# A vision-transformer tokenizer on one Trainium2 core: the unit's steps in another order on TensorE, VectorE, GpSimd and SyncE

## The chip, the cores and the metric

The kernel runs on one NeuronCore of one Trainium2 chip. The metric is the device time of one execution in microseconds (us), lower is better. Engines are named PE (TensorE), DVE (VectorE), ACT (ScalarE), POOL (GpSimd) and SP (SyncE, which issues the DMAs). Each engine runs its own instructions in program order, and they wait for each other through semaphores that only count upwards.

## The reference

The program is a tokenizer for 64 images of 64 channels and 64 by 64 pixels, then a linear oscillator scan over 256 tokens per image, a GELU/SiLU mixing, a mixture of experts, and two layer norms. The change touches only the tokenizer, which is this:

```python
x = features.reshape(b, c, h, s, w, s)                # s = 4: patches of 16 pixels
reduce_feats = x.mean((3, 5)).reshape(b, c, hw).transpose(0, 2, 1)
unf = x.transpose(0, 1, 2, 4, 3, 5).reshape(b, c, hw, n).transpose(0, 2, 3, 1)
q = _ln(reduce_feats, ln_q_w, ln_q_b) @ Wq.T
kv = _ln(unf, ln_kv_w, ln_kv_b) @ Wkv.T
attn = jax.nn.softmax(jnp.einsum('bhpd,bhpnd->bhpn', q * scale, k), axis=-1)
aggre = jnp.einsum('bhpn,bhpnd->bhpd', attn, v)
aggre = aggre.transpose(0, 2, 1, 3).reshape(b, hw, c)
return reduce_feats + aggre @ proj_w.T + proj_b
```

Each patch's mean is the query, its 16 pixels are keys and values, and the result is projected and added to the mean.

## The kernel before, in words

The tokenizer takes 32 units (`UNITS`) of two images each, one image in partitions 0 to 63, the other in 64 to 127. A unit's pixels (2 MB) lie in one of four slots (`NF`) of `arena`, seen as `x[:, m, b, c]`: two halves b of four chunks c of 512 columns. Step n works on four units at once: it makes keys and scores of unit n+1, values of unit n, the projection of unit n-1, and means, squares and query of unit n+2. The order is written out by hand for each engine.

PE, step n (L1020 ff.), in program order: `keys(n+1, c)` for c = 0 to 3 (four matmuls each, into slot c % 2 of a ring of two PSUM buffers), `project(n-1, part)` for part = 0, 1, 2 (16 matmuls each, reading `prodv` of unit n-1), `scores(n+1)`, `values(n, k)` for k = 0 to 3 (same ring, slot k % 2), and for unit n+2 `pixel_squares`, `query` and `pixel_means`. Below, K0 to K3, P0 to P2, S, V0 to V3, SQ, Q and MS stand for these groups. Their waits:

- K2 and K3 wait until DVE has taken K0 and K1 from the ring (`keys_times_q`); S waits for all four key products.
- V0 waits for the third key product of unit n+1 (ring slot 0 was K2's), V1 for the fourth; V2 and V3 wait for the value products of V0 and V1 (`values_weighted`).
- P0 waits for all four value products of unit n-1; P2 waits for `pixels_added`, POOL's four additions of unit n-1.
- Q waits for `tokens_ready` of unit n-1, since both lie in the PSUM tile `qp`.

DVE, step n (L1475 ff.): four `key_products(n+1, c)` (KP0 to KP3), `tokens(n-1)`, `score_scale(n+1)`, `score_max(n+1)`, `value_products(n, 0)` and 1 (VP0, VP1), `score_sum(n+1)`, `query_var(n+2)`, `score_inverse(n+1)`, VP2, `query_scaled(n+2)`, VP3, `pixel_var(n+2)`. `prodv`, the result of the value products, has one buffer: VP0 of unit n may overwrite it only once P2 of unit n-1 has read it. That is one line of `value_products`:

```python
                if k == 0:
                    dve.wait_ge(projected_mm, u)
```

`projected_mm` counts the P2 groups that are done, so with u = n this is P2 of unit n-1. `tokens(n-1)` waits for the same count.

POOL, step n (L605 ff.): `patch_sums_first(n+2)` (waits for the pixels of that unit), `add_pixels(n-1, 2)` and `(n-1, 3)`, three smaller sums, `shift_scores(n+1)` (waits for `score_max`), `add_pixels(n, 0)`, `weigh_scores(n+1)` (waits for ACT's exponential), `add_pixels(n, 1)`, `norm_scores(n+1)`. `add_pixels(u, k)` needs VPk of unit u.

SP, step n: eight DMAs of 256 KB that spread the weights of unit n+1 over the partitions (`spread_weights`, from `wgt` to `wbc`, after `norm_scores`), then two DMAs of 1 MB that load unit n+4, which wait for V3 of unit n. ACT's order is not touched: for a unit it has squares, means, `expo(n+1)`, then `q_square`, `q_rstd`, `query` of n+2.

Of the kernel before, what the change touches and what calls it, by code (L numbers as in the profile page):

```python
# [35 lines left out]
UNITS = PAIRS  # L36
# [6 lines left out]
NF = 4  # L43
# [60 lines left out]
def build(nc, t):  # L104

    ctx = ExitStack()
    with ctx:
# [201 lines left out]
        def count(value):  # L309

            return max(value, 0) if isinstance(value, int) else value
# [180 lines left out]
        def patch_sums_first(eng, u, m):  # L492

            eng.wait_ge(x_in[m], x_count(u, m))
            pix = x[:, m].rearrange("p b c (n i) -> p (b c) n i", i=G32)
            eng.wait_ge(patch_summed, u)
            eng.tensor_tensor(rows[:, :, :, :], pix[:, :, 0:8], pix[:, :, 8:16], ALU.add).then_inc(sum8_ready, 1)  # L497
# [23 lines left out]
        @block.sync  # L521
        def _(sp):
            def load(u):

                m = u % NF
                sp.wait_ge(values_mm, count((u - NF) * NC + NC))
                for b in range(2):
                    sp.dma_start(x[:, m, b].rearrange("p c n -> p (c n)"),
                                 t["x"][u][:, b * (PX // 2):(b + 1) * (PX // 2)]
                                 ).then_inc(x_first_half if isinstance(u, int) and u == 0 and b == 0 else x_in[m], 16)  # L530

            def spread_weights(u):

                sp.wait_ge(weights_ready, u + 1)
                for k in range(0, NC, 2):
                    sp.wait_ge(values_weighted, count(NC * (u - 1) + k + 2))
                    for i in range(2):
                        for c in VALUE_ORDER[k:k + 2]:
                            sp.dma_start(wbc[:, c, i, :],  # L539
                                         wgt[32 * c + i:32 * c + 32:2, None, :].to_broadcast([16, D, CH])  # L540
                                         ).then_inc(weights_spread[c], 16)

            sp.dma_start(tok_w[:, :], t["tok_w"]).then_inc(tok_in, 16)
            sp.dma_start(const[:, 0:K_SEL], t["const"][:, 0:K_SEL]).then_inc(const_in, 16)
            load(0)
            for u in range(1, NF):
                load(u)
            sp.dma_start(rest_w[:, :], t["rest_w"]).then_inc(rest_in, 16)
            sp.dma_start(const[:, K_SEL:K_END], t["const"][:, K_SEL:K_END]).then_inc(select_in, 16)
            spread_weights(0)  # L550
            for n in range(UNITS):
                if n + 1 < UNITS:
                    spread_weights(n + 1)
                if n + NF < UNITS:
                    load(n + NF)

            def store(i, p):
                sp.wait_ge(out_ready, i + 1)
                sp.dma_start(t["out"][i], out_t[:, p].rearrange("p a n -> p (a n)")).then_inc(stored[p], 16)

            with sp.Fori(0, ITERS // 2) as k:
                for p in range(2):
                    store(2 * k + p, p)
            for p in range(2):
                sp.wait_ge(stored[p], STORE * (ITERS // 2))
# [3 lines left out]
        def _(pool):  # L569
# [16 lines left out]
            def norm_scores(u):  # L586
                pool.wait_ge(weights_raw, u + 1)
                pool.wait_ge(inverse_sum_ready, u + 1)
                pool.tensor_tensor(scores_of(wgt), scores_of(wgt), by_patch(srz), ALU.mult).then_inc(weights_ready, 1)  # L589

            def add_pixels(u, k):

                c = VALUE_ORDER[k]
                pool.wait_ge(values_weighted, NC * u + k + 1)
                part = prodv[:, :, :, G32 * c:G32 * (c + 1)]
                pool.tensor_tensor(part[:, :, N_SUM - N_PRE:N_SUM], part[:, :, N_SUM - N_PRE:N_SUM], part[:, :, N_SUM:N_PIX],  # L596
                                   ALU.add).then_inc(pixels_added, 1)
# [3 lines left out]
            shift_scores(0)  # L601
            weigh_scores(0)
            norm_scores(0)

            def step(n, m):  # L605
                prev = not isinstance(n, int) or n >= 1
                nxt = not isinstance(n, int) or n + 1 < UNITS
                nxt2 = not isinstance(n, int) or n + 2 < UNITS
                if nxt2:
                    patch_sums_first(pool, n + 2, (m + 2) % NF)  # L610
                if prev:
                    add_pixels(n - 1, 2)
                    add_pixels(n - 1, 3)
                if nxt2:
                    patch_sums_rest(pool, n + 2)
                if nxt:
                    shift_scores(n + 1)
                add_pixels(n, 0)
                if nxt:
                    weigh_scores(n + 1)  # L620
                add_pixels(n, 1)
                if nxt:
                    norm_scores(n + 1)

            pipeline(pool, step, UNITS)
            add_pixels(UNITS - 1, 2)
            add_pixels(UNITS - 1, 3)


# [255 lines left out]
        def _(pe):  # L885
# [66 lines left out]
            def keys(u, m, c):  # L952

                if c >= 2:
                    pe.wait_ge(keys_times_q, NC * u + c - 1)
                elif u <= 1:
                    pe.wait_ge(keys_times_q, count(NC * u - 1 + c))
                else:
                    pe.wait_ge(values_weighted, NC * (u - 2) + 3 + c)
                pe.wait_ge(weights_centred, 1)  # L960
                quarter(c % 2, c, wqkv[:, 1, :], m).then_inc(keys_mm, 1)
# [58 lines left out]
            def step(n, m):  # L1020
                prev, nxt, nxt2 = n >= 1, n + 1 < UNITS, n + 2 < UNITS
                m1, m2 = (m + 1) % NF, (m + 2) % NF
                if nxt:
                    keys(n + 1, m1, 0)
                    keys(n + 1, m1, 1)
                if prev:
                    project(n - 1, 0)
                if nxt:
                    keys(n + 1, m1, 2)
                if prev:  # L1030
                    project(n - 1, 1)
                if nxt:
                    keys(n + 1, m1, 3)
                if prev:
                    project(n - 1, 2)
                if nxt:
                    scores(n + 1)
                values(n, m, 0)
                values(n, m, 1)
                if nxt2:  # L1040
                    pixel_squares(n + 2, m2)
                    query(n + 2, m2)
                elif nxt:
                    pe.wait_ge(rest_in, 16)
                    pe.wait_ge(variance_ready, UNITS)
                    pe.wait_ge(scores_scaled, UNITS)
                    drive(0, 0)
                values(n, m, 2)
                values(n, m, 3)
                if nxt2:  # L1050
                    pixel_means(n + 2, m2)

            def last_step(n, m):
                drive(0, 1)
# [214 lines left out]
        def _(dve):  # L1269
# [205 lines left out]
            def step(n, m):  # L1475
                nxt = not isinstance(n, int) or n + 1 < UNITS
                nxt2 = not isinstance(n, int) or n + 2 < UNITS
                m1 = (m + 1) % NF
                if nxt:
                    for c in range(NC):  # L1480
                        key_products(n + 1, m1, c)
                if not nxt:
                    for j in range(1, EARLY):
                        scan_ahead(0, j)
                        scan_on(0, j)
                if not isinstance(n, int) or n >= 1:
                    tokens(n - 1, (m - 1) % NF)
                if nxt:
                    score_scale(n + 1)
                    score_max(n + 1)  # L1490
                value_products(n, m, 0)
                value_products(n, m, 1)
                if nxt:
                    score_sum(n + 1)
                if nxt2:
                    query_var(n + 2)
                if nxt:
                    score_inverse(n + 1)
                if not nxt:
                    for level in range(3):  # L1500
                        far_steps(level)
                value_products(n, m, 2)
                if nxt2:
                    query_scaled(n + 2)
                value_products(n, m, 3)
                if nxt2:
                    pixel_var(n + 2)
                if not nxt:
                    for j in range(EARLY, BEFORE_TOKENS):
                        scan_ahead(0, j)  # L1510
                        scan_on(0, j)
# [262 lines left out]
```

## Time and profile before

| | us |
|---|---|
| Median of 3 runs | 903.9 (899.05 to 904.35) |
| The profiled execution | 902.04 |
| its span (first to last instruction) | 900.2 |
| PE busy | 849.0 (94%) |
| DVE busy | 724.7 (81%) |
| POOL busy | 524.5 (58%) |
| ACT busy | 494.1 (55%) |
| mean granted TensorE clock | 0.991 of full speed |

Span and time of the profiled execution differ by 1.84 us, which lies around the span. Busy is the sum over an engine's instructions. The tokenizer fills the first 575 us or so; behind it POOL is nearly idle and there are next to no DMAs. In a timeline row the first number is the start in us, the second the time that the group lasts, and "x16" the number of instructions in it. PE runs each matmul of this kernel as two instructions, so K0 alone is a row of x8 and a projection part one of x32. Rows that follow each other overlap by 0.04 to 0.18 us, since an instruction starts before the one ahead of it has drained: from start to start is then the step that counts.

### The profile page before, as it was taken

Reading aid. Unit: us, or ns where it says so; the run is one execution under the profiler, and the core shown is the slowest. Engines: PE = TensorE matmul, PEld = TensorE weight load, DVE = VectorE, ACT = ScalarE, POOL = GpSimd, SP = SyncE. Lnnn points to the kernel's source line nnn. Section 1 sums busy time; section 2 is a strip of 40 time slices with the busy share of each in tenths; the row PEclk is TensorE's granted clock in tenths of the full one; section 3 lists DMA queues with packets and bytes.
Section 4 is the critical chain, followed back from the end, with each engine's and each line's share of the span. In section 5 each row is a group of like instructions: output and inputs, shape, how many; then the busy total and the mean of one; then the engine's idle time right before and its main releaser. Section 6 shows DMA issues by size and latency. Waiting matters only on the chain.

```text
span 900.2 us, 23485 instructions
## 1 busy us (share of the span) xinstructions
PE 849.0 (94%) x9144; PEld 354.6 (39%) x9144; DVE 724.7 (81%) x1189; ACT 494.1 (55%) x782; POOL 524.5 (58%) x387
## 2 busy tenths in 40 slices
PE   4799999999999999999999999798999999999996
PEld 1234334334334334334334334355344444444442
DVE  5688888788788788788788788894878878778775
ACT  3555455455445545545545556455756666666662
POOL 2799989989999999999989993200212112111110
PEclk9999999999999999999999999898999999999999
DMA  9578888988988887987987965200000000000000
GB/s 358 179 196 231 241 279 227 249 275 226 249 275 224 254 274 216 254 279 224 250 278 224 251 185 137 52 2 2 1 12 13 24 13 13 24 12 13 24 13 35
DMA packets 49057, 141.60 MB, mean 157 GB/s; under 512 B 5441, under 2 KB 5441, under 8 KB 40769
## 3 DMA queue, kind: packets, MB, share of 16 engines
q1 hardware_dynamic: 48960, 140.21, 52.6%
q8 instruction: 74, 1.21, 0.6%
q14 instruction: 23, 0.18, 0.1%
HBM read 68.88 MB, written 4.19 MB: 81 GB/s over the span
## 4 chain that ended last, share of the span: by engine, by line
PE 45%; POOL 23%; issue 13%; DMA 8%; SPq 5%; DVE 4%; ACT 1%; POOLq 1%; DVEq 0%
DMA sb_arena<-x 7%; PE ring L948 6%; POOL sb_prodv L596 5%; PE ring L1207 4%; POOL sb_rows L502 4%; SPq L539 4%; PE ring L1177 4%; PE bank_ms L920 3%; PE bank_ms L1219 3%; POOL sb_wgt L589 3%; POOL sb_score L578 3%; POOL sb_wgt L584 3%; POOL sb_rows L504 2%; PE qp L1162 2%; PE qp L987 2%
## 5 line engine op out<-in xcount | busy, mean ns | idle before, releaser
L948 PE MATMUL ring<-sb_arena,sb_wqkv 64*64 64x512 f32 x2048 | 255.1, 601 | 5.2 <-DVE sb_prodv L1380 3.8
L1349 DVE TENSOR_TENSOR sb_prodk<-ring,sb_qbuf 128x1024 f32<-128x1024 f32 x128 | 153.3, 1220 | 18.5 <-PE ring L948 15.3
L645 POOL TENSOR_TENSOR sb_parts_q<-sb_arena,sb_const 128x512 fp32r<-128x512 f32 x15 | 15.6, 1041 | 247.4 <-DVE sb_arena L1585 194.3
L497 POOL TENSOR_TENSOR sb_rows<-sb_arena 128x2048 f32<-128x2048 f32 x31 | 141.9, 4576 | 28.0 <-DMA sb_arena<-x 27.8
L1380 DVE TENSOR_TENSOR sb_prodv<-ring,sb_wbc 128x1024 f32<-128x1024 f32 x128 | 150.9, 1201 | 1.9 <-issue 1.9
L689 ACT ACTIVATE sb_xsq<-sb_arena 128x2048 f32<-128x2048 f32 x64 | 118.4, 1896 | 3.6 <-DMA sb_arena<-x 3.6
L987 PEld LDWEIGHTS qp<-sb_prodv,sb_tok_w 64*64 64x64 f32 x3072 | 89.0, 133 | 71.2 <-POOL sb_prodv L596 33.7
L948 PEld LDWEIGHTS ring<-sb_arena,sb_wqkv 64*64 64x64 f32 x2048 | 65.7, 132 | 119.0 <-issue 93.9
L987 PE MATMUL qp<-sb_prodv,sb_tok_w 64*64 64x128 f32 x3072 | 101.9, 271 | 10.5 <-POOL sb_prodv L596 8.7
L596 POOL TENSOR_TENSOR sb_prodv<-sb_prodv 128x256 f32<-128x256 f32 x128 | 93.2, 741 | 11.0 <-DVE sb_prodv L1380 11.0
L660 ACT ACTIVATE sb_means<-sb_sum 128x256 f32<-128x256 f32 x32 | 13.3, 416 | 117.1 <-POOL sb_sum L507 115.0
L502 POOL TENSOR_TENSOR sb_rows<-sb_rows 128x1024 f32<-128x1024 f32 x31 | 73.9, 2383 | 0.2
L920 PE MATMUL bank_ms<-sb_prodk,sb_const 128*32 128x512 f32 x512 | 61.6, 598 | 7.5 <-DVE sb_prodk L1349 6.9
L920 PE MATMUL bank_ms<-sb_arena,sb_const 128*32 128x512 f32 x512 | 63.3, 613 | 2.2 <-DVE sb_bqkv L1323 2.2
L920 PE MATMUL bank_sq<-sb_xsq,sb_const 128*32 128x512 f32 x512 | 61.5, 598 | 0.0
L578 POOL TENSOR_TENSOR sb_score<-sb_score,sb_smx 128x512 f32<-128x512 f32 x32 | 41.2, 1289 | 29.6 <-DVE sb_smx L1363 29.6
L1356 DVE TENSOR_TENSOR sb_score<-bank_ms,sb_rstd 128x512 f32<-128x512 f32 x32 | 22.1, 692 | 40.8 <-PE bank_ms L920 40.8
L450 ACT ACTIVATE sb_arena<-ring,sb_rest_w 128x512 f32<-128x512 f32 x72 | 48.9, 682 | 7.7 <-PE ring L1167 2.9
L1177 PE MATMUL ring<-sb_arena,sb_rest_w 64*128 64x512 f32 x144 | 48.6, 614 | 0.0
L584 POOL TENSOR_TENSOR sb_wgt<-sb_score,sb_rstd 128x512 f32<-128x512 f32 x32 | 41.0, 1281 | 8.6 <-ACT sb_score L705 7.4
L1207 PE MATMUL ring<-sb_prodk,sb_rest_w 128*64 128x512 f32 x192 | 45.9, 598 | 0.0
L589 POOL TENSOR_TENSOR sb_wgt<-sb_wgt,sb_srz 128x512 f32<-128x512 f32 x32 | 41.3, 1289 | 0.9 <-DVE sb_srz L1372 0.9
(248 smaller groups left out, 1448.2 us busy)
## 6 DMA issues: line engine op xcount, KB each, us to landing
sb_arena<-x SPq DMA_DIRECT2D x64, 1024.0 KB, 8.6
sb_wbc<-sb_wgt SPq DMA_DIRECT2D x256, 256.0 KB, 4.9
out<-sb_arena SPq DMA_DIRECT2D x16, 256.0 KB, 2.0
sb_rest_w<-rest_w SPq DMA_DIRECT2D x1, 950.5 KB, 22.6
sb_const<-const SPq DMA_DIRECT2D x1, 264.5 KB, 3.1
sb_tok_w<-tok_w SPq DMA_DIRECT2D x1, 260.5 KB, 3.0
sb_const<-const SPq DMA_DIRECT2D x1, 256.0 KB, 22.8
```

The lines of the kernel that those rows point to most:

```text
L497: eng.tensor_tensor(rows[:, :, :, :], pix[:, :, 0:8], pix[:, :, 8:16], ALU.add).then_inc(sum8_ready, 1)
L502: eng.tensor_tensor(rows[:, :, 0:4], rows[:, :, 0:4], rows[:, :, 4:8], ALU.add).then_inc(sum4_ready, 1)
L589: pool.tensor_tensor(scores_of(wgt), scores_of(wgt), by_patch(srz), ALU.mult).then_inc(weights_ready, 1)
L596: pool.tensor_tensor(part[:, :, N_SUM - N_PRE:N_SUM], part[:, :, N_SUM - N_PRE:N_SUM], part[:, :, N_SUM:N_PIX], ALU.add).then_inc(pixels_a ...
L689: act.activation(xsq[:, half], x[:, m, b].rearrange("p c n -> p (c n)"), ACT.Square).then_inc(pixels_squared, 1)
L920: mm = pe.matmul(bank[32 * c:32 * c + 32, :], what, src[c], start=(b == 0), stop=(b == 1))
L948: mm = pe.matmul(ring[slot][C * half:C * half + C, i, :], image_block(w, i), x[C * i:C * i + C, m, half, c], start=True, stop=True)
L987: mm = pe.matmul(qp[C * i:C * i + C, half, 3 * PT:4 * PT], image_block(projw, half), prodv[rows_of, i, n, :], start=(n == 0), stop=(n == N ...
L1177: pe.matmul(pair[m][:, :], ew1[rows, e, :], h2[rows, i % 3, :], start=True, stop=True).then_inc(ring_mm, 1)
L1207: mm = pe.matmul(bank[C * h:C * h + C, :], ew2[:, 2 * q + h, :], h1e[:, im, 2 * q + h], start=True, stop=True)
L1349: dve.tensor_tensor(by_pixel(prodk[:, c]), by_pixel(ring[c % 2][:, :, :]), q[:, :, None, :].to_broadcast([P, 2, N_PIX, G32]), ALU.mult).th ...
L1380: dve.tensor_tensor(prodv[:, :, :, G32 * c:G32 * (c + 1)], by_pixel(ring[k % 2][:, :, :]), by_pixel(wbc[:, c]), ALU.mult).then_inc(values_ ...
```

## The change

It reorders steps; no computation is added or removed.

- PE: the order in a step becomes K0, P0, K1, P1, K2, K3, V0, S, P2, V1, V2, Q, SQ, MS, V3. Before it was K0, K1, P0, K2, P1, K3, P2, S, V0, V1, SQ, Q, V2, V3, MS.
- DVE: KP0 to KP3, VP0, `score_scale`, `tokens`, `score_max`, VP1, VP2, `query_var`, `score_sum`, `score_inverse`, `query_scaled`, VP3, `pixel_var`.
- POOL: `add_pixels(n, 2)` and `patch_sums_first(n+3)` end step n. So of the two additions that stood behind the first sum, one stands ahead of it.
- SP: the load of a unit is split by chunks and not by halves. Its first DMA (chunks 0 and 2 of both halves) is issued ahead of the spread, after V1; the second (chunks 1 and 3) behind the spread, after V3. Each still moves 1 MB, in runs of 512 numbers (2 KB) where there were runs of 2048 (8 KB).

```diff
@@ SP
+            def load_chunks(u, first):
+
+                m = u % NF
+                sp.wait_ge(values_mm, (u - NF) * NC + 2 * (first + 1))
+                sp.dma_start(x[:, m, :, first::2, :], t["x"][u].rearrange("p (b c n) -> p b c n", b=2, c=NC)[:, :, first::2, :]
+                             ).then_inc(x_in[m], 16)
...
             for n in range(UNITS):
+                if n + NF < UNITS:
+                    load_chunks(n + NF, 0)
                 if n + 1 < UNITS:
                     spread_weights(n + 1)
                 if n + NF < UNITS:
-                    load(n + NF)
+                    load_chunks(n + NF, 1)
@@ POOL, step
-                if nxt2:
-                    patch_sums_first(pool, n + 2, (m + 2) % NF)
                 if prev:
-                    add_pixels(n - 1, 2)
                     add_pixels(n - 1, 3)
...
+                add_pixels(n, 2)
+                if nxt3:
+                    patch_sums_first(pool, n + 3, (m + 3) % NF)
@@ PE, step
                 if nxt:
                     keys(n + 1, m1, 0)
-                    keys(n + 1, m1, 1)
                 if prev:
                     project(n - 1, 0)
                 if nxt:
-                    keys(n + 1, m1, 2)
+                    keys(n + 1, m1, 1)
                 if prev:
                     project(n - 1, 1)
                 if nxt:
+                    keys(n + 1, m1, 2)
                     keys(n + 1, m1, 3)
+                values(n, m, 0)
+                if nxt:
+                    scores(n + 1)
                 if prev:
                     project(n - 1, 2)
-                if nxt:
-                    scores(n + 1)
-                values(n, m, 0)
                 values(n, m, 1)
+                values(n, m, 2)
                 if nxt2:
+                    query(n + 2, m2)
                     pixel_squares(n + 2, m2)
-                    query(n + 2, m2)
+                    pixel_means(n + 2, m2)
...
-                values(n, m, 2)
                 values(n, m, 3)
-                if nxt2:
-                    pixel_means(n + 2, m2)
@@ DVE, step (n + 1 < UNITS), behind the four key_products
+                    value_products(n, m, 0)
+                    score_scale(n + 1)
+                    if not isinstance(n, int) or n >= 1:
+                        tokens(n - 1, (m - 1) % NF)
+                    score_max(n + 1)
+                    value_products(n, m, 1)
+                    value_products(n, m, 2)
+                    if nxt2:
+                        query_var(n + 2)
+                    score_sum(n + 1)
+                    score_inverse(n + 1)
+                    if nxt2:
+                        query_scaled(n + 2)
+                    value_products(n, m, 3)
+                    if nxt2:
+                        pixel_var(n + 2)
```

How PE's instructions stand, before, from P0 of a step to S: `qp<-sb_prodv` is a projection part, `ring<-sb_arena` a quarter of keys or values, `bank_ms<-sb_prodk` the scores. (The line numbers are those of each kernel's own code, 9 higher behind SP's part after the change.)

```order
L987 MATMUL qp<-sb_prodv,sb_tok_w 64x128 [waits q_scaled,weights_scaled,tokens_ready,values_weighted]
L987 MATMUL qp<-sb_prodv,sb_tok_w 64x128 x15
L948 MATMUL ring0<-sb_arena,sb_wqkv 64x512 [waits weights_centred,keys_times_q]
L948 MATMUL ring0<-sb_arena,sb_wqkv 64x512 x3
L987 MATMUL qp<-sb_prodv,sb_tok_w 64x128 x16
L948 MATMUL ring1<-sb_arena,sb_wqkv 64x512 [waits weights_centred,keys_times_q]
L948 MATMUL ring1<-sb_arena,sb_wqkv 64x512 x3
L987 MATMUL qp<-sb_prodv,sb_tok_w 64x128 [waits pixels_added]
L987 MATMUL qp<-sb_prodv,sb_tok_w 64x128 x15
L920 MATMUL bank_ms<-sb_prodk,sb_const 32x512 [waits mean_squared,keys_times_q]
```

The same place after the change, from P1 to P2:

```order
L996 MATMUL qp<-sb_prodv,sb_tok_w 64x128 x16
L957 MATMUL ring0<-sb_arena,sb_wqkv 64x512 [waits weights_centred,keys_times_q]
L957 MATMUL ring0<-sb_arena,sb_wqkv 64x512 x3
L957 MATMUL ring1<-sb_arena,sb_wqkv 64x512 [waits weights_centred,keys_times_q]
L957 MATMUL ring1<-sb_arena,sb_wqkv 64x512 x3
L957 MATMUL ring0<-sb_arena,sb_wqkv 64x512 [waits weights_centred,keys_times_q]
L957 MATMUL ring0<-sb_arena,sb_wqkv 64x512 x3
L929 MATMUL bank_ms<-sb_prodk,sb_const 32x512 [waits mean_squared,keys_times_q]
L929 MATMUL bank_ms<-sb_prodk,sb_const 32x512 x7
L996 MATMUL qp<-sb_prodv,sb_tok_w 64x128 [waits pixels_added]
```

The third projection part moved from ahead of the scores to behind them, K2 and K3 now follow each other, and V0 stands right behind them.

DVE before, from the last key product of a step (`prodk`) to `query_var`: `hT` is `tokens`, `score` is `score_scale`, `smx` is `score_max`, `prodv` a value product, `ssm` is `score_sum`.

```order
L1349 TENSOR_TENSOR sb_prodk<-ring1,sb_qbuf 128x1024 [waits keys_mm]
L1387 ISA [waits projected_mm]
L1387 SCALAR_TENSOR_TENSOR sb_hT<-qp,sb_bqkv,sb_means 128x16x16
L1356 TENSOR_TENSOR sb_score<-bank_ms,sb_rstd 128x512 [waits weights_raw,rstd_ready,scores_mm]
L1363 TENSOR_REDUCE sb_smx<-sb_score 128x32 [waits scores_scaled]
L1377 REGISTER_ALU [waits values_mm]
L1380 TENSOR_TENSOR sb_prodv<-ring0,sb_wbc 128x32x32 [waits projected_mm,weights_spread0]
L1380 TENSOR_TENSOR sb_prodv<-ring1,sb_wbc 128x32x32 [waits weights_spread2,values_mm]
L1367 TENSOR_REDUCE sb_ssm<-sb_score 128x32 [waits scores_exp]
```

The same place after:

```order
L1357 TENSOR_TENSOR sb_prodk<-ring1,sb_qbuf 128x1024 [waits keys_mm]
L1385 REGISTER_ALU [waits values_mm]
L1388 TENSOR_TENSOR sb_prodv<-ring0,sb_wbc 128x32x32 [waits projected_mm,weights_spread0]
L1364 TENSOR_TENSOR sb_score<-bank_ms,sb_rstd 128x512 [waits weights_raw,rstd_ready,scores_mm]
L1395 ISA [waits projected_mm]
L1395 SCALAR_TENSOR_TENSOR sb_hT<-qp,sb_bqkv,sb_means 128x16x16
L1371 TENSOR_REDUCE sb_smx<-sb_score 128x32 [waits scores_scaled]
L1388 TENSOR_TENSOR sb_prodv<-ring1,sb_wbc 128x32x32 [waits weights_spread2,values_mm]
```

The first value product moved from behind `tokens`, `score_scale` and `score_max` to ahead of them, and kept its wait for `projected_mm`.

## Rows read from the trace of the kernel before

**Rows 1.** Busy time in stretches: length, then each engine's busy us (x instructions).

```profile
core 0: us, PE busy (x) PEld busy (x) DVE busy (x) ACT busy (x) POOL busy (x), PEclk, DMA share, GB/s
50.27:541.55 491.28, 478.10 (x6500) 189.31 (x6496) 413.37 (x465) 253.38 (x349) 450.53 (x321) 1.00 0.84 245
```

**Rows 2.** Waits over that stretch, PE and POOL: us in total, times, longest.

```profile
PE qp L987 <- POOL sb_prodv L596: 8.7, 15, 1.3
...
POOL sb_rows L497 <- DMA sb_arena<-x: 11.0, 20, 1.5
```

**Rows 3.** Timeline of PE in one unit: start us, us, group, [idle before <-releaser].

```profile
322.51 1.95 PE L948 MATMUL ring<-sb_arena,sb_wqkv 64*64 64x512 f32 x16
324.28 1.05 PE L987 MATMUL qp<-sb_prodv,sb_tok_w 64*64 64x128 f32 x32
325.16 1.09 PE L948 MATMUL ring<-sb_arena,sb_wqkv 64*64 64x512 f32 x8
326.07 1.05 PE L987 MATMUL qp<-sb_prodv,sb_tok_w 64*64 64x128 f32 x32
326.94 1.04 PE L948 MATMUL ring<-sb_arena,sb_wqkv 64*64 64x512 f32 x8
328.41 1.10 PE L987 MATMUL qp<-sb_prodv,sb_tok_w 64*64 64x128 f32 x32 [0.43 <-POOL sb_prodv L596]
329.44 1.92 PE L920 MATMUL bank_ms<-sb_prodk,sb_const 128*32 128x512 f32 x16
331.30 1.95 PE L948 MATMUL ring<-sb_arena,sb_wqkv 64*64 64x512 f32 x16
...
335.03 0.66 PE L908 MATMUL qp<-sb_means,sb_const 64*64 64x256 f32 x8
...
335.73 1.90 PE L948 MATMUL ring<-sb_arena,sb_wqkv 64*64 64x512 f32 x16
```

**Rows 4.** Timeline of DVE in the same unit.

```profile
328.05 1.23 DVE L1349 TENSOR_TENSOR sb_prodk<-ring,sb_qbuf 128x1024 f32<-128x1024 f32 x1 [0.51 <-PE ring L948]
...
329.69 0.69 DVE L1387 SCALAR_TENSOR_TENSOR sb_hT<-qp,sb_bqkv,sb_means 128x256 f32 x1 [0.42 <-PE qp L987]
...
331.44 0.69 DVE L1356 TENSOR_TENSOR sb_score<-bank_ms,sb_rstd 128x512 f32<-128x512 f32 x1 [1.05 <-PE bank_ms L920]
...
332.16 1.05 DVE L1363 TENSOR_REDUCE sb_smx<-sb_score 128x32 f32<-128x512 f32 x1
...
333.12 2.34 DVE L1380 TENSOR_TENSOR sb_prodv<-ring,sb_wbc 128x1024 f32<-128x1024 f32 x2
...
335.39 1.05 DVE L1367 TENSOR_REDUCE sb_ssm<-sb_score 128x32 f32<-128x512 f32 x1
...
336.40 0.43 DVE L1328 TENSOR_TENSOR sb_qstat<-qp,sb_qstat 128x256 f32<-128x256 f32 x1
...
336.74 0.34 DVE L1372 RECIPROCAL sb_srz<-sb_ssm 128x32 f32<-128x32 f32 x1
...
338.08 0.41 DVE L1333 TENSOR_TENSOR sb_qraw<-qp,sb_qrstd 128x256 f32<-128x256 f32 x1
...
338.41 1.21 DVE L1380 TENSOR_TENSOR sb_prodv<-ring,sb_wbc 128x1024 f32<-128x1024 f32 x1
...
340.18 0.69 DVE L1338 TENSOR_TENSOR sb_vstat<-bank_sq,sb_vstat 128x512 f32<-128x512 f32 x1 [0.56 <-ACT sb_vstat L694]
```

**Rows 5.** Timeline of POOL and ACT in the same unit.

```profile
333.29 1.29 POOL L578 TENSOR_TENSOR sb_score<-sb_score,sb_smx 128x512 f32<-128x512 f32 x1 [0.35 <-DVE sb_smx L1363]
...
334.61 0.64 ACT L705 ACTIVATE sb_score<-sb_score 128x512 f32<-128x512 f32 x1 [0.92 <-POOL sb_score L578]
...
335.98 0.39 ACT L666 ACTIVATE sb_qstat<-qp 128x256 f32<-128x256 f32 x1 [0.73 <-PE qp L913]
```

**Rows 6.** Busy time of a stretch with loads only, then of the tokenizer's end.

```profile
10.00:20.00 10.00, 6.91 (x54) 2.39 (x58) 6.30 (x16) 5.48 (x7) 2.75 (x1) 1.00 1.01 425
...
550.00:600.00 50.00, 42.74 (x629) 21.76 (x626) 46.10 (x105) 19.19 (x34) 12.37 (x16) 0.93 0.20 47
```

**Rows 7.** Timeline of PE at the tokenizer's end: two value quarters after a long wait.

```profile
565.78 3.10 PE L948 MATMUL ring<-sb_arena,sb_wqkv 64*64 64x512 f32 x16 [3.22 <-DVE sb_prodv L1380]
```

More of the change, by code:

```diff
@@ L525, in load @@
                 m = u % NF
-                sp.wait_ge(values_mm, count((u - NF) * NC + NC))
                 for b in range(2):
@@ L603, in _ @@
             norm_scores(0)
+            patch_sums_first(pool, 2, 2)
             def step(n, m):
@@ L608, in step @@
                 nxt2 = not isinstance(n, int) or n + 2 < UNITS
-                if nxt2:
-                    patch_sums_first(pool, n + 2, (m + 2) % NF)
+                nxt3 = not isinstance(n, int) or n + 3 < UNITS
                 if prev:
-                    add_pixels(n - 1, 2)
                     add_pixels(n - 1, 3)
@@ L623, in step @@
                     norm_scores(n + 1)
+                add_pixels(n, 2)
+                if nxt3:
+                    patch_sums_first(pool, n + 3, (m + 3) % NF)
             pipeline(pool, step, UNITS)
-            add_pixels(UNITS - 1, 2)
             add_pixels(UNITS - 1, 3)
@@ L1481, in step @@
                         key_products(n + 1, m1, c)
-                if not nxt:
+                    value_products(n, m, 0)
[14 more added lines that the diff above has]
+                        pixel_var(n + 2)
+                else:
                     for j in range(1, EARLY):
@@ L1485, in step @@
                         scan_on(0, j)
-                if not isinstance(n, int) or n >= 1:
                     tokens(n - 1, (m - 1) % NF)
[L1488 to L1499, printed above, removed]
+                    value_products(n, m, 0)
+                    value_products(n, m, 1)
                     for level in range(3):
                         far_steps(level)
[L1502 to L1508, printed above, removed]
+                    value_products(n, m, 2)
+                    value_products(n, m, 3)
                     for j in range(EARLY, BEFORE_TOKENS):
```

## The prediction, as it stood before the changed kernel ran

> **What bounds the kernel now.** I read the busy times of the tokenizer first [rows 1]. The stretch from the K0 of step 1 (50.27) to the K0 of step 30 (541.55) holds 29 steps of 491.28 / 29 = 16.94 us. In one step PE is busy for 478.1 / 29 = 16.49 us, POOL 15.54, DVE 14.25. So three engines lie close together: PE has 0.45 us to spare, POOL 1.4, DVE 2.69. Then the waits [rows 2]: PE loses 8.7 us over the stretch to POOL's pixel additions ahead of P2, and POOL 11.0 us to pixels that are still landing. These two are what the new order takes aim at. Last the timeline of one step [rows 3 to 5], from which every step time below is read: [rows 3] for PE, [rows 4] for DVE, [rows 5] for POOL and ACT. The reader should see in [rows 4] that DVE's idle is spread over four short waits (0.51, 0.42, 1.05, 0.56), and that none of them is for `projected_mm` in a value product.
>
> **What the change can give.** P2 behind S no longer waits for POOL, and the first half of a load starts earlier. If nothing else moved, the step would come down to PE's busy time, 16.49: a gain of at most 0.45 x 29 = 13 us. A load that is issued as two interleaved halves costs SP nothing that counts (it has idle time), and its first DMA is issued ahead of the spread, not into it.
>
> **What it adds.** Two waits, both worked out from program order and [rows 3, 4].
>
> First, K2 is now followed by K3 and V0 alone. V0 needs the third key product (KP2). K2 to the start of its product takes 328.05 - 326.94 = 1.11 us (K3's rows, the same shape), the product 1.23, and DVE's end to PE's start 329.44 - (328.05 + 1.23) = 0.16. So V0 starts no earlier than 2.50 after K2, where K2 and K3 fill only 1.8: PE waits 0.7. S then needs KP3: 1.11 + 2 x 1.23 + 0.16 = 3.73 after K2, and V0 ends its 0.9 at 3.4: PE waits 0.3. Before, this place lost 0.43.
>
> Second, and this decides: VP0 of unit n is now the next thing behind KP3 on DVE, and it waits for P2 of unit n-1 (`projected_mm`). P2 is now behind S, and S is behind KP3. So DVE must stand still from the end of KP3 until S and P2 are through: 0.16, then S 331.30 - 329.44 = 1.86, then from P2's start to DVE's 329.69 - 328.41 = 1.28: 3.30 us, in every step, with everything behind VP0 queued up: `score_scale` (whose scores are ready), `tokens`, `score_max`, and by `score_max` the whole softmax on POOL and ACT. DVE had only 2.69 us to spare.
>
> **The new step, walked once round.** Time 0 is the start of VP3 of one unit.
> - VP3 1.21, then 0.16 to PE: P0 at 1.37.
> - P0, K1, P1 at 0.88, 0.91, 0.87 (differences of starts in [rows 3]): K2 at 4.03. DVE has `pixel_var` 0.69, KP0 and KP1 2.46 to do meanwhile, which fits before KP2.
> - KP2 at 4.03 + 1.11 = 5.14; KP3 ends 2.46 later, at 7.60.
> - DVE idle 3.30: VP0 at 10.90.
> - VP0 to the next at 2.27 / 2 = 1.14 (two products from 333.12 to 335.39): 12.04. `score_scale` 0.69, `tokens` 0.69: `score_max` at 13.42.
> - On PE: Q waits for `tokens`, so it starts at 13.42 + 0.16 = 13.58; then 0.70 (335.03 to 335.73), SQ and MS at 1.86 each as S: V3 at 18.00, and VP3 of the next unit 1.11 later, at 19.1.
> - On DVE: from `score_max` to POOL's shift 1.13, to the exponential 1.32, its own 0.64, then `q_square` to `query_var` 0.42 [rows 4, 5]: `query_var` at 16.93. Then 0.34, `score_sum` 1.05, inverse 0.34, `query_scaled` 0.33 (338.08 to 338.41): VP3 can start at 18.99.
>
> The two branches nearly tie at 19.0 to 19.1. Rows overlap by up to 0.07, so I take 19.05, or 2.11 us above 16.94. POOL (15.54) and PE (16.49) fit inside.
>
> **The sum.** 29 steps x 2.11 = 61.2. In step 30 the order is the same, and the weights of the last unit hang on `score_max`: before, it starts 332.16 - 322.51 = 9.65 after K0; now K0 starts 0.9 behind V3, at 18.00 + 0.9 - 19.05 = -0.15, and `score_max` comes 13.57 after it, 3.9 later. Step 0 has no projection, only the first added wait: 0.5. Together 65.6. The profiled execution took 902.04, so 967.6; its time is 1.9 below the median 903.9, which is less than the spread of the three runs, so I forecast **968 us**. The stages behind the tokenizer are not touched.
>
> **The edits costed at nothing.** POOL's reordering: VP2 is there before `norm_scores` is through, and POOL gets 3.5 us of slack per step. The loads: before, pixels came 11.0 us of waiting too late over 20 steps [rows 2], and now they start earlier relative to a longer step. Their cost in DMA time is not in the trace, which has them only as 8 KB runs: 425 GB/s at a full share [rows 6], so 2.1 MB take 4.9 us of a step. The spread, in 2 KB runs, must be the rest of 0.84 x 16.94 = 14.2: 9.3 us for as many bytes [rows 1]. The new loads lie between: 14.2 if their runs cost nothing, 18.6 if they cost what the spread's do. Both are below 19.05, the upper one barely. I take no cost, since the landing of pixels has whole steps of slack, and keep the upper end for the range.
>
> **Rivals.**
> - *Part of the wait is absorbed (5%).* The forced 3.30 us replace DVE's other waits fully, and KP2 isn't held up by P0: 14.25 + 3.30 = 17.55 a step, 0.61 more, 29 x 0.61 + 3.9 = 22: 924 us. Against it: from VP3's end (1.21) to KP2 (5.14) the way goes through P0, K1, P1 and K2 and takes 3.93 us, in which DVE has 3.15 us of work, so 0.78 stand still as well; and Q's wait for `tokens` holds SQ, MS and V3.
> - *DMA becomes the bound (6%).* The 2 KB loads cost more than the spread's runs, or disturb it so that value products wait for `wbc`. It decides from 19.05 - 9.3 = 9.8 us for a unit's pixels, twice the present 4.9. At 20.5 a step: 44 us more, 1010.
> - *TensorE's clock falls (4%).* PE is now idle about 2.6 us of a step in five gaps. In the trace the granted clock is 1.00 over all 29 steps, and 0.93 in the stretch at the end [rows 6], where after an idle of 3.22 two quarters take 3.10 [rows 7] instead of 1.95 [rows 3], so for the most part at 1.2 and not at 2.4 GHz. No gap here comes to 3.22: the longest is V2's, which waits for VP0 (12.11 + 0.16, where P2 and V1 end near 11.4), 0.85. About 12 us of the walk are PE's; at 1.6 times that is 7 us for each step at the low level, and 7 such steps give 50 us: 1018. The Trainium skill (TensorE: Matmul & The Clock Gate, "A second HAM failure mode: psum-queue depth-cycling") has a kernel whose PE idled shortly and often between groups and whose clock went up and down; by this rule the sum would be that of this rival. The trace before, with one short wait a step, doesn't show it.
> - *The other side: not slower (2%).* The mechanism is the one aimed at: P2 without POOL's wait and pixels earlier, down to PE's 16.49, or 891 us. It decides only if VP0's wait costs DVE less than its slack, 2.69 - (16.94 - 16.49) = 2.2 us. S and P2 alone are 3.1, so the wait would have to be met by something else than P2 of unit n-1, which the counter's one increment per P2 excludes. If only that wait were void, `score_scale` would still wait for S and `tokens` for P2, and the step would be about 17.3, some 913 us.
> - *The rest (the forecast's mechanism): 83%.* Its own range is 18.33 a step (DVE's busy 14.25, the 3.30, and the 0.78 of the way over P0) to 19.6 (all steps at busy times without overlap, and waits for the 2 KB loads): 29 x 1.39 + 4 = 44 and 29 x 2.66 + 5 = 82, so 946 to 984.
>
> **How the numbers follow.** The range of 940 to 988 holds the forecast's cases and leaves out the absorbed wait, DMA, clock and no loss, together somewhat under 2 in 10. A measurement of this kernel can tell about 1% from no change. Faster by over 1% has 1%, within 1% 2%, slower 97%.
>
> **What would show it.** A step (K0 to K0) of 19 us in the timeline; DVE idle before the first value product of each step, some 3.3 us, released by PE `qp` (the projection), about 30 times, so 95 to 100 us in the waits; PE waits before V0 (0.7), S (0.3), V2 (for VP0) and Q (for `tokens`); POOL waiting for `score_max` some 3 us a step and hardly for pixels; PE's wait for POOL's additions gone. DVE's busy time unchanged at 14.25 a step. It would be wrong if the DVE wait were there, but the step short of 18.3 (then another order of waits hides it), or if the spread's or the loads' landing appeared as the releaser.

## The result

The changed kernel takes 957.59 us (median of 4 runs, 956.15 to 957.98) against 902.65 us of the kernel before (4 runs): a ratio of 1.061 (95% interval 1.058 to 1.064), 55 us slower. The forecast was 968, its range 940 to 988.

### The profile page after: what moved, and what is told of

Read it like the earlier page. It is cut to its first block, busy times and chain, and to the rows that moved or that the text cites. A ratio compares the mean times of both kernels' runs of the same rounds, so it can differ in the third digit from the quotient of the medians.

```text
span 954.4 us, 23485 instructions
## 1 busy us (share of the span) xinstructions
PE 858.8 (90%) x9144; PEld 354.2 (37%) x9144; DVE 721.1 (76%) x1189; ACT 487.3 (51%) x782; POOL 523.1 (55%) x387
## 2 busy tenths in 40 slices
DMA packets 70560, 141.60 MB, mean 148 GB/s; under 512 B 5440, under 2 KB 5440, under 8 KB 69440
## 3 DMA queue, kind: packets, MB, share of 16 engines
q1 hardware_dynamic: 70464, 140.21, 51.1%
## 4 chain that ended last, share of the span: by engine, by line
POOL 34%; PE 31%; issue 27%; DVE 4%; ACT 1%; DMA 1%; POOLq 1%; SPq 1%; DVEq 0%
POOL sb_prodv L604 8%; POOL sb_rows L502 7%; PE ring L1215 4%; POOL sb_score L586 4%; POOL sb_rows L504 4%; POOL sb_rows L497 4%; POOL sb_wgt L592 3%; PE ring L1185 3%; PE bank_ms L1227 3%; POOL sb_sum L507 2%; PE qp L1170 2%; PE bank_sq L1215 1%; PE bank_ms L1222 1%; PE ring L1130 1%; PE bank_ms L1185 1%
## 5 line engine op out<-in xcount | busy, mean ns | idle before, releaser
L957 PE MATMUL ring<-sb_arena,sb_wqkv 64*64 64x512 f32 x2048 | 260.8, 602 | 37.6 <-DVE sb_prodv L1388 21.6
L1388 DVE TENSOR_TENSOR sb_prodv<-ring,sb_wbc 128x1024 f32<-128x1024 f32 x128 | 153.2, 1217 | 116.1 <-PE qp L996 94.7
L996 PEld LDWEIGHTS qp<-sb_prodv,sb_tok_w 64*64 64x64 f32 x3072 | 85.9, 133 | 86.4 <-DVE sb_prodv L1388 44.2
L714 ACT ACTIVATE sb_score<-sb_score 128x512 f32<-128x512 f32 x32 | 20.3, 633 | 106.0 <-POOL sb_score L586 106.0
L707 ACT ACTIVATE sb_vstat<-sb_vstat,sb_const 128x512 f32<-128x512 f32 x32 | 23.1, 722 | 42.7 <-DVE sb_vstat L1346 42.6
```

The lines of the kernel that those rows point to most:

```text
L957: mm = pe.matmul(ring[slot][C * half:C * half + C, i, :], image_block(w, i), x[C * i:C * i + C, m, half, c], start=True, stop=True)
L996: mm = pe.matmul(qp[C * i:C * i + C, half, 3 * PT:4 * PT], image_block(projw, half), prodv[rows_of, i, n, :], start=(n == 0), stop=(n == N ...
L1388: dve.tensor_tensor(prodv[:, :, :, G32 * c:G32 * (c + 1)], by_pixel(ring[k % 2][:, :, :]), by_pixel(wbc[:, c]), ALU.mult).then_inc(values_ ...
```

## The profile after

The profile page's busy times and the head of its groups, where the loss stands in one line:

```profile
span 954.4 us, 23485 instructions
...
PE 858.8 (90%) x9144; PEld 354.2 (37%) x9144; DVE 721.1 (76%) x1189; ACT 487.3 (51%) x782; POOL 523.1 (55%) x387
...
L957 PE MATMUL ring<-sb_arena,sb_wqkv 64*64 64x512 f32 x2048 | 260.8, 602 | 37.6 <-DVE sb_prodv L1388 21.6
L1388 DVE TENSOR_TENSOR sb_prodv<-ring,sb_wbc 128x1024 f32<-128x1024 f32 x128 | 153.2, 1217 | 116.1 <-PE qp L996 94.7
```

The value products' line on the page of before, to lay beside the last one:

```profile
L1380 DVE TENSOR_TENSOR sb_prodv<-ring,sb_wbc 128x1024 f32<-128x1024 f32 x128 | 150.9, 1201 | 1.9 <-issue 1.9
```

The work is the same (23485 instructions, DVE 721 us busy where it was 725), the span 54.2 us longer. DVE idled 116.1 us ahead of the value products (L1388), and 94.7 of them were ended by PE's projection; before, no product waited for it.

The same stretch as [rows 1], K0 of step 1 to K0 of step 30, in busy times and in DVE's, PE's and POOL's waits (us in total, times, longest):

```profile
51.58:595.04 543.46, 489.41 (x6500) 189.29 (x6496) 408.25 (x464) 245.72 (x347) 445.93 (x319) 1.00 0.78 220
```

```profile
DVE sb_prodv L1388 <- PE qp L996: 91.5, 29, 3.2
DVE sb_prodk L1357 <- PE ring L957: 25.0, 58, 0.5
DVE sb_prodv L1388 <- PE ring L957: 17.2, 29, 2.1
...
PE ring L957 <- DVE sb_prodv L1388: 16.3, 29, 0.6
PE ring L957 <- DVE sb_prodk L1357: 14.2, 29, 0.5
PE qp L996 <- DVE sb_prodv L1388: 14.2, 29, 0.5
PE qp L917 <- DVE sb_hT L1395: 8.1, 29, 0.3
...
POOL sb_score L586 <- DVE sb_smx L1371: 83.0, 29, 4.4
```

29 steps of 543.46 / 29 = 18.74 us, where they were 16.94 [rows 1]. DVE waits 91.5 / 29 = 3.16 us in each for P2. PE's waits are the four that the walk named: V2 for VP0 (16.3), V0 for KP2 (14.2), P0 for VP3 (14.2), Q for `tokens` (8.1). PE's wait for POOL's additions and POOL's for pixels [rows 2] are gone; POOL now waits 83.0 us for `score_max`, where it waited 15.9 before. So the two waits that the change takes aim at went away, and the step is 1.80 us longer all the same.

One step on PE and on DVE, to lay beside [rows 3, 4]:

```profile
313.08 1.95 PE L957 MATMUL ring<-sb_arena,sb_wqkv 64*64 64x512 f32 x16
315.52 1.10 PE L996 MATMUL qp<-sb_prodv,sb_tok_w 64*64 64x128 f32 x32 [0.49 <-DVE sb_prodv L1388]
...
318.18 1.90 PE L957 MATMUL ring<-sb_arena,sb_wqkv 64*64 64x512 f32 x16
320.56 1.09 PE L957 MATMUL ring<-sb_arena,sb_wqkv 64*64 64x512 f32 x8 [0.49 <-DVE sb_prodk L1357]
321.69 1.92 PE L929 MATMUL bank_ms<-sb_prodk,sb_const 128*32 128x512 f32 x16
323.55 1.10 PE L996 MATMUL qp<-sb_prodv,sb_tok_w 64*64 64x128 f32 x32
...
326.07 1.09 PE L957 MATMUL ring<-sb_arena,sb_wqkv 64*64 64x512 f32 x8 [0.56 <-DVE sb_prodv L1388]
327.44 0.66 PE L917 MATMUL qp<-sb_means,sb_const 64*64 64x256 f32 x8 [0.28 <-DVE sb_hT L1395]
...
331.82 1.95 PE L957 MATMUL ring<-sb_arena,sb_wqkv 64*64 64x512 f32 x16
```

```profile
314.24 1.23 DVE L1388 TENSOR_TENSOR sb_prodv<-ring,sb_wbc 128x1024 f32<-128x1024 f32 x1 [0.53 <-PE ring L957]
...
319.28 2.36 DVE L1357 TENSOR_TENSOR sb_prodk<-ring,sb_qbuf 128x1024 f32<-128x1024 f32 x2 [0.51 <-PE ring L957]
324.79 1.23 DVE L1388 TENSOR_TENSOR sb_prodv<-ring,sb_wbc 128x1024 f32<-128x1024 f32 x1 [3.15 <-PE qp L996]
325.93 0.68 DVE L1364 TENSOR_TENSOR sb_score<-bank_ms,sb_rstd 128x512 f32<-128x512 f32 x1
326.52 0.65 DVE L1395 SCALAR_TENSOR_TENSOR sb_hT<-qp,sb_bqkv,sb_means 128x256 f32 x1
327.02 1.00 DVE L1371 TENSOR_REDUCE sb_smx<-sb_score 128x32 f32<-128x512 f32 x1
...
332.07 0.36 DVE L1341 TENSOR_TENSOR sb_qraw<-qp,sb_qrstd 128x256 f32<-128x256 f32 x1
332.97 1.23 DVE L1388 TENSOR_TENSOR sb_prodv<-ring,sb_wbc 128x1024 f32<-128x1024 f32 x1 [0.55 <-PE ring L957]
```

The order of events is the walk's: KP3 ends at 321.64, S runs 321.69 to 323.55, P2 from 323.55, VP0 at 324.79. The last two rows show what holds the next VP3: not DVE's own work, which is through at 332.43, but V3 on PE (331.82).

**Where the 54.2 us are**: 29 steps x 1.80 = 52.2; the start up to K0 of step 1, 51.58 - 50.27 = 1.3; from K0 of step 30 to the end of the tokenizer (the first cast of `rest_w` on POOL, at 631.49 and 574.76) 36.45 - 33.21 = 3.2; and behind that, where nothing was changed, 322.9 - 325.4 = -2.5.

## The experiments

Steps are read from the timelines as (start of the 32nd scores group - start of the third) / 29: 16.90 us before, 18.74 after. "Against before" is the ratio to runs of the kernel before on the same chip, with its 95% interval.

| Kernel | Median us | Against before | Step us |
|---|---|---|---|
| Changed | 957.59 | 1.061 (1.058 to 1.064) | 18.74 |
| 1. Changed, P2 ahead of S | 917.18 | 1.018 (1.014 to 1.021) | 17.36 |
| 2. Changed, VP0 freed of P2 | 917.77 | 1.017 (1.012 to 1.021) | 17.43 |
| 3. Changed, softmax ahead of VP0 | 958.45 | 1.063 (1.059 to 1.067) | 18.79 |
| 4. Changed, loads as before | 957.66 | 1.061 (1.056 to 1.066) | 18.74 |
| 5. As 1, and keys as before | 905.19 | 1.005 (1.003 to 1.007) | 16.98 |
| 6. As 5, and V3 ahead of MS | 899.67 | 0.998 (0.997 to 0.999) | 16.82 |
| 7. As 6, and another order on DVE | 892.97 | 0.989 (0.985 to 0.993) | 16.62 |
| 8. Before, with the new loads | 897.89 | 0.996 (0.995 to 0.998) | 16.79 |
| 9. Before, with POOL's part | 899.75 | 0.999 (0.997 to 1.000) | 16.85 |
| 10. Before, with both | 897.73 | 0.997 (0.996 to 0.999) | 16.79 |

**1. P2 ahead of the scores.** One thing undone:

```diff
                 values(n, m, 0)
-                if nxt:
-                    scores(n + 1)
                 if prev:
                     project(n - 1, 2)
+                if nxt:
+                    scores(n + 1)
```

> The changed kernel with one thing undone on PE: P2 of unit n-1 stands between V0 and S again, not behind S. DVE, POOL and SP as changed. Forced wait: VP0 then waits only until V0 (1.13 us) and P2 (1.24) are through, about 1.3 us behind KP3's end and not 3.15; score_scale then waits for S, tokens follow, and Q starts some 1.2 us earlier, behind V2. Step 17.5 instead of 18.74, time about 922 us, DVE's wait for the projection under 50 us in place of 94.7. Rival, the chain on PE (tokens, Q, SQ, MS, V3 in a row) binds by itself: step stays above 18.4, over 948 us. Rival, the 2 KB loads: 957 us, nothing changes.

It took 917.18 us. DVE's waits, the whole program:

```profile
DVE sb_prodv L1388 <- PE qp L996: 30.9, 30, 1.1
...
DVE sb_score L1364 <- PE bank_ms L929: 18.7, 31, 2.0
```

The wait for the projection falls from 94.7 to 30.9 us, and 40 of the 55 us are back. The rivals "PE's row alone" (over 948) and "the loads" (957) fall. The time is 5 us below the 922 that I expected; VP0's wait for P2 was 1.1 us at most, not 1.3.

**2. The cause taken away, the order kept.**

```diff
+                            src = prodv[rows_of, i, n, :] if part < 2 or u >= UNITS - 2 else const[rows_of, 0:PT]
...
-                                           prodv[rows_of, i, n, :], start=(n == 0), stop=(n == N_SUM - 1))
+                                           src, start=(n == 0), stop=(n == N_SUM - 1))
+                if part == 1:
+                    mm.then_inc(two_parts_mm, 1)
...
                 if k == 0:
-                    dve.wait_ge(projected_mm, u)
+                    dve.wait_ge(two_parts_mm, u)
```

> The changed kernel with its order kept, but the cause of the wait taken away: P2 of units 0 to 29 reads a constant tile instead of prodv (so the third part of the projection is wrong), and VP0 waits for P1 and not for P2. Forced wait: VP0 starts behind V0, within 0.2 us of KP3's end; score_scale then waits for S (about 2 us from its start), tokens for P2, and PE's own order S, P2, V1, V2, Q lets Q start 1.2 us earlier. Step about 17.5, time about 922 us. Rival, the chain on PE binds by itself: over 948 us. Rival, the loads: 957 us. If the forced wait were the whole of the loss, the step would be 16.9 and the time 903 us; I expect that the new place of V0 and the row from Q to V3 keep 0.6 us a step.

In units 0 to 29 the third part of the projection reads a constant tile, so what it should add to the result is left out; the number and the shape of the instructions stay. It took 917.77 us, as the first to 0.6 us, though P2 is still behind S. DVE's timeline in one step:

```profile
318.18 2.36 DVE L1361 TENSOR_TENSOR sb_prodk<-ring,sb_qbuf 128x1024 f32<-128x1024 f32 x2 [0.51 <-PE ring L958]
320.78 1.23 DVE L1392 TENSOR_TENSOR sb_prodv<-ring,sb_wbc 128x1024 f32<-128x1024 f32 x1 [0.24 <-PE ring L958]
322.58 0.69 DVE L1368 TENSOR_TENSOR sb_score<-bank_ms,sb_rstd 128x512 f32<-128x512 f32 x1 [0.58 <-PE bank_ms L930]
323.74 0.67 DVE L1399 SCALAR_TENSOR_TENSOR sb_hT<-qp,sb_bqkv,sb_means 128x256 f32 x1 [0.47 <-PE qp L998]
...
330.57 1.23 DVE L1392 TENSOR_TENSOR sb_prodv<-ring,sb_wbc 128x1024 f32<-128x1024 f32 x1 [0.91 <-PE ring L958]
```

VP0 starts 0.24 us behind KP3, where it was 3.15; in its place DVE waits 0.58 for the scores and 0.47 for P2. Only what VP0 waits for was changed, with the tile that P2 reads, so the forced wait is shown to be the cause of 40 us. A stall of 3.15 us a step cost 1.31 (18.74 - 17.43). Most of the rest is taken by other waits once it is gone: the three just named, and VP3's for V3, 0.91 in place of 0.55. The prediction's last rival had worked out this very case ("if only that wait were void") at a step of about 17.3 and 913 us; it came to 17.43 and 918.

**3. The softmax out of the queue behind VP0.**

```diff
-                    value_products(n, m, 0)
                     score_scale(n + 1)
+                    score_max(n + 1)
+                    value_products(n, m, 0)
                     if not isinstance(n, int) or n >= 1:
                         tokens(n - 1, (m - 1) % NF)
-                    score_max(n + 1)
```

> The changed kernel with DVE's score_scale and score_max ahead of VP0 and tokens, so that the softmax is no longer queued up behind the waiting VP0. PE's order as changed, P2 still behind S. The walk says that it is not the softmax that the step waits for but V2 (waits for VP0) and Q (waits for tokens), then Q, SQ, MS, V3: score_max now ends only after P2 is through, VP0 starts 0.5 us later, and so do V2, Q and VP3: step 19.0 in place of 18.74, 966 us. Rival, what is queued behind VP0 (scores, softmax, spread of the weights) is the path: these start 2 us earlier, the step falls by 0.6 or more, 940 us or less.

It took 958.45 us. PE and DVE in one step:

```profile
326.80 0.69 DVE L1364 TENSOR_TENSOR sb_score<-bank_ms,sb_rstd 128x512 f32<-128x512 f32 x1 [2.04 <-PE bank_ms L929]
327.52 1.04 DVE L1371 TENSOR_REDUCE sb_smx<-sb_score 128x32 f32<-128x512 f32 x1
328.49 1.20 DVE L1388 TENSOR_TENSOR sb_prodv<-ring,sb_wbc 128x1024 f32<-128x1024 f32 x1
...
329.75 1.09 PE L957 MATMUL ring<-sb_arena,sb_wqkv 64*64 64x512 f32 x8 [1.12 <-DVE sb_prodv L1388]
```

The rival falls: `score_max` starts 2.7 us behind S (324.81) where it was 5.3 (327.02 - 321.69), and it brings nothing. V2 waits 1.12 for VP0 in place of 0.56, and Q follows 0.91 behind V2 without a wait, so in this order it is V2, and behind it PE's row Q, SQ, MS, V3, that the step hangs on; in the changed kernel Q still waits 0.28 for `tokens`. My 966 was too high by 7.5: Q started only 0.1 us later than in the changed kernel (5.85 us behind S against 5.75), since it no longer waits for `tokens`.

**4. The loads as before.** Two halves in 8 KB runs, both behind the spread.

```diff
-                if n + NF < UNITS:
-                    load_chunks(n + NF, 0)
                 if n + 1 < UNITS:
                     spread_weights(n + 1)
                 if n + NF < UNITS:
-                    load_chunks(n + NF, 1)
+                    load(n + NF)
```

> The changed kernel with the loads as before: two halves in 8 KB runs, both behind the spread and V3. Forced wait: DVE and PE set the step, pixels have slack; 957 us, within 3. Rival, the 2 KB loads cost DMA time that the step feels: 5 us or more faster. Other rival, the early first half is a gain hidden in the result: 5 us or more slower, with POOL waiting for pixels.

It took 957.66 us against 957.59: no difference, in either direction.

**5 and 6. The keys' order, then V3's place**, on top of the first. Experiment 5 puts K0 K1 P0 K2 P1 K3 back ahead of V0 P2 S; experiment 6 also V3 ahead of MS.

```diff
                     keys(n + 1, m1, 0)
+                    keys(n + 1, m1, 1)
                 if prev:
                     project(n - 1, 0)
                 if nxt:
-                    keys(n + 1, m1, 1)
+                    keys(n + 1, m1, 2)
                 if prev:
                     project(n - 1, 1)
                 if nxt:
-                    keys(n + 1, m1, 2)
                     keys(n + 1, m1, 3)
```

> P2 ahead of S (917 us, step 17.42), and also the keys as before: K0 K1 P0 K2 P1 K3, then V0 P2 S. The place of K2: P1 stands between K2 and K3 again, so that KP2 is through when V0 comes. V0's wait of 0.5 us and S's go, and P0 is moved behind K1, which takes some of its wait for VP3: step 17.05, 907 us. Rival, the row from Q to V3 on PE sets the step alone: 917 us as before.

```diff
                     pixel_squares(n + 2, m2)
-                    pixel_means(n + 2, m2)
...
                 values(n, m, 3)
+                if nxt2:
+                    pixel_means(n + 2, m2)
```

> As the kernel with P2 ahead of S and the keys as before, and also V3 ahead of MS. VP3 then starts 1.8 us earlier, but pixel_var waits for MS and the key products behind it: step 16.9, 902 us. What is left to the 893 us of the other new order is then the order of DVE alone (tokens and score_sum earlier). Rival: V3's place is worth nothing, 907 us.

They took 905.19 and 899.67 us. The keys' order, and with it the second added wait of the forecast (K2, K3, V0 in a row), was worth 17.36 - 16.98 = 0.38 us a step, 12 us. The edit also moves P0 behind K1, but that gains nothing: K1 now has the wait for VP3 that P0 had (first row), while K3 and V0 form one row of x16 with no wait between them (second row).

```profile
324.20 1.09 PE L957 MATMUL ring<-sb_arena,sb_wqkv 64*64 64x512 f32 x8 [0.49 <-DVE sb_prodv L1388]
...
327.72 1.90 PE L957 MATMUL ring<-sb_arena,sb_wqkv 64*64 64x512 f32 x16
```

V3 behind SQ and MS cost 0.16 a step, 5.5 us. PE's waits in the last one, in the stretch 50 to 545:

```profile
PE qp L917 <- ACT sb_means L670: 9.0, 25, 0.5
PE qp L996 <- POOL sb_prodv L604: 0.2, 1, 0.2
```

**7. A new order.** As experiment 6, with DVE's `tokens` ahead of `score_scale` and `score_sum` ahead of `query_var`:

```diff
                     value_products(n, m, 0)
-                    score_scale(n + 1)
                     if not isinstance(n, int) or n >= 1:
                         tokens(n - 1, (m - 1) % NF)
+                    score_scale(n + 1)
                     score_max(n + 1)
                     value_products(n, m, 1)
                     value_products(n, m, 2)
+                    score_sum(n + 1)
                     if nxt2:
                         query_var(n + 2)
-                    score_sum(n + 1)
                     score_inverse(n + 1)
```

> A new order: PE K0 K1 P0 K2 P1 K3 V0 P2 S V1 V2 Q SQ V3 MS; DVE KP0 to KP3, VP0, tokens, score_scale, score_max, VP1, VP2, score_sum, query_var, inverse, query_scaled, VP3, pixel_var; POOL and SP as changed. If the place of V0 behind K3 is good as long as K2 stands well ahead of it and P2 stays ahead of S, the step comes near PE's busy time, 16.5: about 891 us, faster than before by 1%. Rival: V0 ahead of S delays the scores by 0.9 us and so the softmax on POOL, which is busy 15.5 us of a step: step 17.2, 911 us.

It took 892.97 us, 0.989 of the kernel before (0.985 to 0.993), and so it is faster than both the kernel before and the changed one. The new loads are in it too; on the kernel before they give 0.996 by themselves (experiment 8), so the larger part comes from the order. Here `tokens` finds P2 done, where `score_scale` has to wait for S anyway. Two of DVE's waits in the stretch 50 to 545, and above them the only one that PE has there:

```profile
PE qp L917 <- ACT sb_means L670: 4.0, 14, 0.4
...
DVE sb_qraw L1342 <- ACT sb_qrstd L682: 22.2, 29, 0.8
DVE sb_prodv L1389 <- PE qp L996: 17.5, 30, 0.6
```

VP0 still waits for P2, but 0.6 us and not 3.2, since P2 is ahead of S. PE is left with 4.0 us of waits in 29 steps, and the step, 16.62, is near PE's busy time, 16.49 in [rows 1].

**8 to 10. What the loads and POOL's part are worth in the old order.** The edits are the SP and POOL parts of the change, on the kernel before.

> The kernel before with only the loads of the change: chunks 0 and 2 in one DMA ahead of the spread, chunks 1 and 3 behind it, in 2 KB runs. In the order before, POOL waits 11 us over 29 steps for pixels and PE 8.7 us for POOL's additions. If the early half helps, POOL's first sum starts up to 0.5 us earlier and the step falls by 0.2: 897 us. If the 2 KB runs cost DMA time, the spread lands later and the time is the same or up to 5 us more. The second half is still issued behind the spread, so I expect little: within 3 us of before.

> The kernel before with only POOL's part of the change: the third addition ahead of the next first sum. POOL's wait for pixels (0.3 to 0.9 us in 20 of 29 steps) is then filled with 0.7 us of work, and the fourth addition, for which P2 waits, comes up to 0.5 us earlier: PE's 8.7 us of waiting go in part, 898 us. If P2's wait were only moved on to S (for KP3), within 2 us of before.

> The kernel before with POOL's part and the loads of the change, PE and DVE as before. Both remove the wait for pixels, so together no more than one alone: 897 us, with PE's waits between K3 and S at 0.4 us a step for KP3, since K3, KP3 and S follow each other there whatever POOL does.

They took 897.89, 899.75 and 897.73 us against 901.32. So the loads are worth 0.4% (0.2 to 0.5%), POOL's part at most 0.3%, and both no more than the loads alone. PE's waits for KP3 ahead of S in the kernel before (the stretch of [rows 2]), then all of PE's waits with the new loads and with POOL's part, in 50 to 545:

```profile
PE bank_ms L920 <- DVE sb_prodk L1349: 3.3, 10, 0.5
```

```profile
PE bank_ms L928 <- DVE sb_prodk L1357: 11.5, 28, 0.5
PE qp L995 <- POOL sb_prodv L604: 1.7, 1, 1.7
```

```profile
PE bank_ms L921 <- DVE sb_prodk L1350: 9.0, 22, 0.5
PE qp L988 <- POOL sb_prodv L596: 4.6, 7, 1.3
```

With the loads PE's 8.7 us of waiting for POOL [rows 2] go to 1.7, but its wait for KP3 ahead of S goes from 3.3 (10 times) to 11.5 (28 times): K3, its product and S follow each other whatever POOL does. Of the 13 us that the forecast gave as the most that these edits can bring, 3.4 are there.

## Why the prediction was right, point by point

- **The forced wait**: right in place, cause and size. 3.30 us forecast, 3.15 in the timeline, 29 times in the 29 steps; experiment 2 shows it as the cause.
- **The way round**: Walk and timeline, from the start of VP3 (314.24): P0 1.37 and 1.28, K2 4.03 and 3.94, KP2 5.14 and 5.04, KP3's end 7.60 and 7.40, VP0 10.90 and 10.55, `score_max` 13.42 and 12.78, Q 13.58 and 13.20, V3 18.00 and 17.58, VP3 19.1 and 18.73. The intervals that came out 0.1 or more too long are those in which I added whole durations or 0.16 us from DVE's end to PE's start. That 0.16 was misread: in [rows 3] S stands right behind P2 with no wait listed, so its start was set by P2 and not by KP3; in the changed kernel S starts 0.05 behind KP3's end (321.64 and 321.69). The term that was most off is `score_scale` and `tokens`: 1.38 forecast, 327.02 - 325.93 = 1.09 measured. Nearly as much was lost again at Q, which starts 327.44 - 327.02 = 0.42 behind `score_max` and not 0.16, so part of the agreement at the end of the walk is two errors of opposite sign.
- **What ends last**: the two branches were taken as a near tie; PE's (Q, SQ, MS, V3) is behind by the 0.55 us that VP3 waits for V3. DVE's own branch, put at 18.99, was through at 332.43 - 314.24 = 18.19.
- **The size**: 2.11 us a step forecast, 1.80 measured. Profiled execution against profiled execution, 967.6 was forecast and 956.15 measured, 11.4 too high: 29 x 0.31 = 9.0 is the step. The last unit was put at 3.9 and came to 3.2, the start at 0.5 and came to 1.3, which cancel. The other 2.5 us lie behind the tokenizer: in its first 70 us there the granted clock was 0.93 before and 0.98 after, at the same work. Over the profiled executions of this study this part took 322.9 to 327.1 us, so it is scatter and no effect of the change.
- **The second added wait**: put at 0.7 and 0.3 us; V0 waits 0.49, and for S the profile lists no wait, though it starts 1.13 behind V0 where a quarter's step is 0.9. The walk didn't separate its worth in the step; the keys' order as a whole is worth 0.38 (experiment 5).
- **Costed at nothing**: right for the loads in this order (experiment 4). POOL's part was never undone by itself in the changed kernel; in the old order it is worth at most 0.3% (experiment 9), so in the new one its nothing is not shown. The price of 2 KB runs lay near the lower end: DMA's share is 0.78 x 18.74 = 14.6 us a step, where the bounds were 14.2 and 18.6.
- **The rivals**: the absorbed wait had something to it. The stall cost 1.31 of its 3.15 us. What the step still has above before without the stall, 17.43 - 16.90 = 0.53, goes with the keys' order (0.38) and V3's place (0.16). DMA as the bound and "not slower" did not come. Nor did the falling clock: it was granted at 1.00 over the 29 steps, with PE busy for 489.41 of 543.46 us and no listed wait longer than 0.6. The Trainium skill (TensorE: Matmul & The Clock Gate, "A second HAM failure mode: psum-queue depth-cycling") tells of a kernel whose clock went up and down with short, frequent gaps between groups; here the trace doesn't agree, with four listed gaps of 0.28 to 0.56 us in a step.

## What to carry to other kernels

Before a step is moved behind another, look up who waits for its end on the other engines, and where in their queues that wait stands: here a single-buffered tile was released by the moved step, and its next writer headed DVE's queue. A wait that costs nothing in the old order, since something ahead of it in the queue waits for the same event anyway (`tokens` did), is invisible in the trace of before and must be read from the code. And the price of a stall isn't its length: walk the new order once round, with start-to-start times, and see which chain closes last; then a fix is tried at the place where it closes.

## What the runs showed of the hardware

- From DVE's end to the start of the PE group that waited for it: 0.05 us for P0 and V2 (VP3 and VP0 end at 315.47 and 326.02, the groups start at 315.52 and 326.07), 0.27 for Q behind `tokens` (327.17 and 327.44).
- The pixels' loads in runs of 2 KB instead of 8 KB, with the order otherwise the same (changed kernel against experiment 4), made 70560 DMA packets where there were 49056, and the DMA queue took 51.1% of the 16 engines' time where it took 49.3%, 0.511 x 954.4 = 488 us against 0.493 x 955.3 = 471. First the changed kernel, then experiment 4:

```profile
DMA packets 70560, 141.60 MB, mean 148 GB/s; under 512 B 5440, under 2 KB 5440, under 8 KB 69440
...
q1 hardware_dynamic: 70464, 140.21, 51.1%
...
sb_arena<-x SPq DMA_DIRECT2D x64, 1024.0 KB, 7.5
```

```profile
q1 hardware_dynamic: 48960, 140.21, 49.3%
...
sb_arena<-x SPq DMA_DIRECT2D x64, 1024.0 KB, 8.6
```

A load of 1 MB landed 7.5 us after its issue in the median, where it took 8.6. The place of the first load's issue differs too, so this isn't the run length alone.
- A group of 16 instructions with tiles of 128x32 goes 1.74 us from start to start when the next group has the same tiles (SQ to MS, 328.25 to 329.99 in the changed kernel), and 1.83 to 1.86 when the next has tiles of 64x64 (MS to V3, 329.99 to 331.82; S to P2, 321.69 to 323.55). No run separates the change of tile from other differences between these groups.
